# Twelve matmuls whose sums nobody reads, at two waits of TensorE in a gated delta layer

## The chip, the cores and the metric

The program runs on one core of a Trainium2 chip. The metric is the device time of one execution in microseconds (us), here 1743.68 us, the median of three runs. TensorE's clock has two levels, 1.2 and 2.4 GHz; the profile prints the granted clock as a share of the full one, so that 0.50 is the lower level and 1.00 the upper one.

## The reference

Eight layers stand one behind the other, each added to the tokens x (1024 tokens of 256 features): attention, a ternary feed-forward net, gated delta, the ternary net again, attention, routed experts, latent attention, routed experts. The change is in gated delta alone (6 heads, keys of 32 and values of 64 numbers, tokens in chunks):

```
q = short_conv(hidden_states @ Wq, conv_wq)      # k and v alike
beta = sigmoid(hidden_states @ Wb)
g = -exp(A_log) * softplus(hidden_states @ Wa + dt_bias)
def _step(S, xs):                                # one token; q and k normed
    S = S * exp(gt)
    pred = einsum('bhk,bhkv->bhv', kt, S)
    delta = (vt - pred) * bt
    S = S + einsum('bhk,bhv->bhkv', kt, delta)
    return S, einsum('bhk,bhkv->bhv', qt, S)
o = o * rsqrt(mean(o * o) + EPS) * norm_weight * silu(gate)
return o @ Wo
```

## The kernel before

A layer is a row of blocks (`nc.Block()`). Inside a block each engine runs its own list in the order in which it is written, and waits where the code says `wait_ge` on a semaphore. At the end of a block all engines meet, so the next one begins when the last of them is through. No scheduler moves anything. Float32 matmuls are shown in the trace as two records each.

Gated delta works on chunks of 128 tokens, 8 for each of the 6 heads. Its blocks that matter here:

- The factor block (L999 to L1080). VectorE makes decays and norms in a long chain, and from L1076 on the scaled copies of q and k: QN, QE, KN, KB, KBE, KD, 8 instructions each, then BV (L1079). TensorE has two small matmuls in it (L1004, L1005) and is then idle.
- The block of P and A (L1099 to L1196). TensorE transposes the sums of g (L1134), which go to DRAM and come back spread over the partitions (L1104, L1107). It transposes KN, KB and QN in six turns of four (L1130), each copied out by ScalarE (L1158), then makes P and A for 12 units b of four chunks (L1146, matmuls over 32 rows); after each of the first ten units stands one more turn. VectorE multiplies P and A by the decays (L1180 to L1195). When six units of A are written, SyncE carries their 32x32 blocks through DRAM (L833, L836), and GpSimd begins on them in the same block (L1119): steps 0 to 17 of a forward substitution with 31 steps (`substitute`, L820 and L824).
- The block of the merges (L1220 to L1339). GpSimd ends its half, and VectorE does the other half of the blocks (L1329). Each half of the finished T blocks goes through DRAM (L842, L1228, L1231), and TensorE merges blocks of 32 to 64 and 128 (L1260 to L1285) and multiplies by KBE (L1250). `swept[n]` counts two for each step of the substitution of half n.

TensorE's list in the block of P and A begins when all engines have left the factor block; its list in the merges begins with a wait for the first half of the T blocks (L1255).

Of the kernel before, what the change touches and what calls it, by code (L numbers as in the profile page):

```python
# [10 lines left out]
ALU = mybir.AluOpType  # L11
# [3 lines left out]
P = 128  # L15
# [4 lines left out]
HALF = 512  # L20
NH2 = S // HALF
HEADS = 16
HD = D // HEADS
LN_EPS = 1e-5


class Core:
# [13 lines left out]
    def sb(self, name, shape, dt, ctx=None):  # L41
        self.n += 1
        return (ctx or self.ctx).enter_context(self.nc.sbuf_tensor(f"{name}_{self.n}", shape, dt))
# [4 lines left out]
    def sem(self, name):  # L48
        self.n += 1
        self.sems.append(self.nc.alloc_semaphore(f"{name}_{self.n}"))  # L50
        return self.sems[-1]
# [39 lines left out]
def norm_stage(nc, core, tag, loads=None, room=None):  # L91
# [8 lines left out]
    with ExitStack() as tmp:  # L100
# [6 lines left out]
        with nc.Block() as block:  # L107
# [6 lines left out]
            def _(dve):  # L114
                for t in range(NT):
                    dve.bn_aggr(mv[:, t, :], core.stats[:, t, :]).then_inc(mv_done, 1)
                dve.wait_ge(mv_done, NT)
                dve.tensor_scalar(ve[:], mv[:, :, 1], LN_EPS, None, ALU.add).then_inc(var_done, 1)
                dve.wait_ge(std_done, 1)
# [636 lines left out]
GH, GK, GV = 6, 32, 64  # L756
# [4 lines left out]
T32 = 32  # L761
# [7 lines left out]
def gated_delta(nc, core, tag, d):  # L769
# [4 lines left out]
    sem = lambda n: core.sem(f"{tag}_{n}")  # L774
    with ExitStack() as tmp:
        sb = lambda n, shape, dt=F32: core.sb(n, shape, dt, tmp)
        SG = sb("silu_gate", [P, NT, VWD])
        KBE = sb("k_beta_eg", [P, NT, GH, GK])
# [10 lines left out]
        with ExitStack() as mid_scope:  # L789
# [15 lines left out]
            t_eye, swept = sem("t_set_to_identity"), [sem(f"swept_{n}") for n in range(NG)]  # L805
# [43 lines left out]
            with ExitStack() as tmp2:  # L849
# [5 lines left out]
                with ExitStack() as tmp3:  # L855
# [27 lines left out]
                    with nc.Block() as block:  # L883
                        @block.sync
                        def _(sp):
                            sp.wait_ge(wload, 32)
                            sp.wait_ge(head_loads, 32)
# [99 lines left out]
                with ExitStack() as tmp3:  # L987
# [7 lines left out]
                    ss, r = sb3("square_sums", [P, NT, 2 * GH]), sb3("inverse_norms", [P, NT, 2 * GH])  # L995
                    fk = EA[:].rearrange("p c n -> p (c n)")[:, 0:5 * NT * GH].rearrange("p (a t h) -> p a t h", a=5, t=NT)
                    ch, aux, from_act, from_pe = sem("chain"), sem("to_act"), sem("from_act"), sem("from_pe")
                    to_pe, sq_done = sem("to_pe"), sem("sq_done")
                    with nc.Block() as block:  # L999
                        @block.tensor  # L1000
                        def _(pe):
                            pe.wait_ge(to_pe, 1)
                            gf = g[:].rearrange("p t h -> p (t h)")
                            pe.matmul(psum[:, 0, 0:NT * GH], tri[:], gf, start=True, stop=True).then_inc(from_pe, 1)  # L1004
                            pe.matmul(psum[:, 1, 0:NT * GH], core.ones_sq[:], gf, start=True, stop=True).then_inc(from_pe, 1)  # L1005

                        @block.scalar
                        def _(act):
# [15 lines left out]
                        def _(dve):  # L1024
                            n = [0]
# [47 lines left out]
                            for out, src, f in ((QN, q, fk[:, 0]), (QE, q, fk[:, 1]), (KN, k, rk), (KB, k, fk[:, 2]),  # L1073
                                                (KBE, k, fk[:, 3]), (KD, k, fk[:, 4])):
                                for t in range(NT):
                                    dve.tensor_tensor(out[:, t], src[:, t, :].rearrange("p (h c) -> p h c", c=GK),  # L1076
                                                      f[:, t, :].unsqueeze(2).broadcast_to([P, GH, GK]), ALU.mult)
                            for t in range(NT):
                                last = dve.tensor_tensor(BV[:, t], YT[:, t, 2 * QKW:].rearrange("p (h c) -> p h c", c=GV),  # L1079
                                                         beta[:, t, :].unsqueeze(2).broadcast_to([P, GH, GV]), ALU.mult)  # L1080
# [122 lines left out]
            with ExitStack() as tmp2:  # L1203
# [11 lines left out]
                bank = lambda b, i: psum[:, 2 * (b % BANKS) + i, 0:CB * T32].rearrange("p (c n) -> p c n", n=T32)  # L1215
# [4 lines left out]
                with nc.Block() as block:  # L1220
# [18 lines left out]
                    def _(pe):  # L1239
# [14 lines left out]
                        def x32(b):  # L1254
                            pe.wait_ge(placed[((b + 1) * CB - 1) // GCH], 16 * 7)  # L1255
                            if b >= BANKS:
                                pe.wait_ge(y64_kept, b - BANKS + 1)
                            for i, c in enumerate(chunks(b)):
                                for q in (0, 2):
                                    last = pe.matmul(bank(b, 0)[group(q + 1), i], EA[group(q), c, group(q + 1)],  # L1260
                                                     T64[group(q), c, 0:T32], start=True, stop=True)
                            last.then_inc(x_in, 1)
# [19 lines left out]
                        def y64(b):  # L1282
                            pe.wait_ge(x64_kept, b + 1)
                            for i, c in enumerate(chunks(b)):
                                last = pe.matmul(half_bank(b)[lo, i], T64[hi, c], TT[hi, c, hi], start=True, stop=True)  # L1285
                            last.then_inc(y64_in, 1)

                        for b in range(NBT + 2):
                            if b < NBT:
                                x32(b)  # L1290
                            if 1 <= b <= NBT:
                                x64(b - 1)
                            if b < NBT:
                                y32(b)
                            if 1 <= b <= NBT:
                                y64(b - 1)
                            if b >= 2:
                                w_features(b - 2)
# [828 lines left out]
```

## Time and profile before

| what | us |
|---|---|
| median of three runs | 1743.68 (1742.83 to 1750.16) |
| the profiled execution | 1737.53 |
| its span | 1735.7 |
| TensorE busy, of the span | 1464.5 |
| VectorE busy | 979.6 |
| ScalarE busy | 662.2 |
| GpSimd busy | 137.3 |

The busy times are shares of one span and overlap. Times in rows are counted from the start of the span. The page's strip of granted clocks has a digit for each 1/40 of the span (43.4 us); gated delta lies in its slices 9 to 15.

### The profile page before, as it was taken

To read this page: it belongs to the slowest core of one execution; us is meant where nothing else is said; L and a number is where in the kernel's file an instruction comes from. 1 tells how busy PE (TensorE), PEld (TensorE's weight loads), DVE (VectorE), ACT (ScalarE), POOL (GpSimd) and SP (SyncE) were. 2 spreads that over 40 slices of the span, in tenths; PEclk is the share of its full clock that TensorE was granted. 3 is DMA by queue.
4 is the path that set the end of the run, shared out by engine and by line. 5 is a ranking of instruction groups with operands and counts; after the bars stand their busy time and mean duration, and the time that the engine had idled before them with its cause. 6 is when DMAs were issued, how large, how long until landed. Compare 5 with 4: busy or idle time off the path is not lost. (4 is left out here: it accounts for less than half of the span.)

```text
span 1735.7 us, 32934 instructions
## 1 busy us (share of the span) xinstructions
PE 1464.5 (84%) x14035; PEld 838.2 (48%) x14035; DVE 979.6 (56%) x2007; ACT 662.2 (38%) x889; POOL 137.3 (8%) x125
## 2 busy tenths in 40 slices
PE   5799994887192895884799997999888999988998
PEld 3255543363182774362255545435334666655435
DVE  4499966744666425652799944432565555534332
ACT  4077781634222211632377752110362333332110
POOL 4000000000016003003000000110130000000110
PEclk9599997898655697897699998999657999997999
DMA  4900002010042200008500002000320000002000
GB/s 115 152 3 3 3 3 73 0 39 0 1 109 50 38 4 0 1 25 151 69 3 3 3 1 86 0 1 1 58 37 10 9 10 10 9 13 76 0 1 25
DMA packets 54952, 51.78 MB, mean 30 GB/s; under 512 B 23843, under 2 KB 41110, under 8 KB 54806
## 3 DMA queue, kind: packets, MB, share of 16 engines
q1 hardware_dynamic: 54806, 49.68, 13.9%
q8 instruction: 111, 1.82, 0.4%
q14 instruction: 35, 0.29, 0.1%
HBM read 36.66 MB, written 9.72 MB: 27 GB/s over the span
## 5 line engine op out<-in xcount | busy, mean ns | idle before, releaser
L453 DVE TENSOR_REDUCE row_max_pieces<-psum 128x1 f32<-128x512 f32 x704 | 425.3, 648 | 145.2 <-PE psum L368 143.5
L519 ACT ACTIVATE probs<-psum 128x1024 f32<-128x1024 f32 (+7 forms) x384 | 343.7, 900 | 297.8 <-PE psum L368 297.7
L425 PE MATMUL psum<-probs,v_ones 128*32 128x256 f32 (+1 forms) x2688 | 238.2, 375 | 2.3 <-ACT out_features L510 1.7
L368 PE MATMUL psum<-q_all,k_head 97*32 97x512 f32 (+3 forms) x1536 | 207.3, 494 | 0.0
L368 PE MATMUL psum<-k_stack,q_stack 96*32 96x512 bf16 x2048 | 174.6, 409 | 27.2 <-PEq L583 26.4
L368 PE MATMUL psum<-q_stack,k_stack 97*32 97x512 bf16 x2048 | 160.0, 384 | 6.6 <-DMA q_stack<-minus_max_rows 6.6
L425 PEld LDWEIGHTS psum<-probs,v_ones 128*32 128x32 f32 x2688 | 85.9, 109 | 59.6 <-issue 14.2
L368 PEld LDWEIGHTS psum<-k_stack,q_stack 96*32 96x32 bf16 x2048 | 59.3, 97 | 101.2 <-issue 29.9
L368 PE MATMUL psum<-k_head_bf,q_all_bf 80*32 80x512 bf16 (+3 forms) x768 | 101.7, 347 | 7.3 <-DMA k_head_bf<-k_features_bf 6.9
L368 PEld LDWEIGHTS psum<-q_stack,k_stack 97*32 97x32 bf16 x2048 | 58.3, 97 | 58.4 <-DMA q_stack<-minus_max_rows 7.6
L1716 DVE TENSOR_TENSOR gate_weighted<-psum,weight_rows 128x512 f32<-128x512 f32 (+1 forms) x48 | 33.1, 690 | 89.4 <-PE psum L1624 89.4
L368 PEld LDWEIGHTS psum<-q_all,k_head 97*32 97x32 f32 x1536 | 71.1, 111 | 15.9 <-issue 1.4
L1657 ACT ACTIVATE silu<-psum 128x512 f32<-128x512 f32 (+1 forms) x48 | 28.6, 596 | 131.3 <-PE psum L1624 131.3
L248 PE MATMUL psum<-xn_parts,w_up_signs 128*128 128x512 bf16 x192 | 49.2, 395 | 20.0 <-DVE xn_parts L295 20.0
L368 PE MATMUL psum<-mask_by_key,identity_bf 128*32 128x128 bf16 x512 | 63.6, 221 | 0.0
L134 ACT ACT_TABLE_LOAD x7 | 9.0, 1283 | 141.2 <-PEq L62 132.1
L368 PE MATMUL psum<-mask_by_query,identity_bf 128*32 128x128 bf16 x512 | 59.2, 231 | 0.0
L368 PEld LDWEIGHTS psum<-k_head_bf,q_all_bf 80*32 80x32 bf16 x768 | 39.4, 99 | 37.9 <-issue 10.4
L1735 PE MATMUL psum<-slot_hidden,down_a 128*128 128x512 f32 (+1 forms) x96 | 47.5, 644 | 6.3 <-PEq L1556 6.3
L1624 PE MATMUL psum<-lora_in,up_b 128*128 128x512 f32 (+1 forms) x96 | 49.9, 601 | 3.4 <-DVE lora_in L1703 3.4
L1848 PE MATMUL psum<-latents,w_q_rotary 64*128 64x512 f32 x64 | 51.0, 977 | 1.2 <-DVE by_cos_over_by_sin L1931 1.2
L151 PE MATMUL psum<-identity,xn 128*128 128x128 f32 x96 | 23.0, 428 | 32.2 <-DVE xn L124 32.2
(334 smaller groups left out, 2286.6 us busy)
## 6 DMA issues: line engine op xcount, KB each, us to landing
aa_parts<-qk_parts SPq DMA_DIRECT2D x12, 256.0 KB, 12.5
q_stack<-aa_parts SPq DMA_DIRECT2D x12, 256.0 KB, 8.5
k_stack<-aa_parts SPq DMA_DIRECT2D x12, 256.0 KB, 17.7
e_then_minus_a<-gd_g_sums SPq DMA_DIRECT2D x6, 512.0 KB, 7.3
ac_parts<-qk_parts SPq DMA_DIRECT2D x12, 256.0 KB, 11.9
q_stack<-ac_parts SPq DMA_DIRECT2D x12, 256.0 KB, 8.7
k_stack<-ac_parts SPq DMA_DIRECT2D x12, 256.0 KB, 18.6
w_up<-in_r_up SPq DMA_DIRECT2D x2, 704.0 KB, 4.7
```

The lines of the kernel that those rows point to most:

```text
L134: act.activation(std[:], ve[:], ACT.Sqrt).then_inc(std_done, 1)
L151: last = pe.transpose(psum[:, 2 * half + f, i * P:(i + 1) * P], xn[:, t, f * P:(f + 1) * P], ident[:])
L248: last = pe.matmul(psum[:, 2 * b + j, :], w[:, k, e * P:(e + 1) * P], XP[:, part, k, cols(half)], start=(part == 0 and k == 0), stop=(part ...
L368: last = pe.matmul(o[j:j + 32], by[:, j:j + 32], rows, **flags)
L425: last = pe.matmul(psum[32 * g:32 * g + VW, PVB, a - g * D:D], V[:, c, h, :], pr[:, n % PB, a:(g + 1) * D], start=(c == 0), stop=(c == (2 ...
L453: dve.reduce_max(mx[:, h % 2, qt, i:i + 1], psum[:, RB + n % RING, 0:b - a], AX.X).then_inc(ring_out, 1)
L519: act.activation(pr[:, n % PB, q_from(c):], psum[:, 2 * (n % 2):2 * (n % 2) + 2, :].rearrange("p a n -> p (a n)")[:, q_from(c):], ACT.Exp, ...
L1624: pe.matmul(psum[0:n, 2 * (p % BUF) + j, :], w[wl][:, a:a + n], Z[:, j, k, cols], start=False, stop=True, skip_group_check=True).then_inc( ...
L1657: act.activation(sil[0:n, i % 2, :], psum[0:n, 2 * (p % BUF), :], ACT.Silu).then_inc(silu, 1)
L1716: dve.tensor_tensor(gc[0:n, i % 2, :], psum[0:n, 2 * (p % BUF) + 1, :], CB[0:n, k, cols], ALU.mult).then_inc(gated, 1)
L1735: last = pe.matmul(psum[:, 2 * half + k, :], w["dnA"][0:n, f, :], H[0:n, k, f, half * HALF:(half + 1) * HALF], start=(f == 0), stop=(f == ...
L1848: last = pe.matmul(o, wq[:, n - 1, :], L[0:LAT, cols(half)], start=True, stop=True)
```

## The change

A helper issues n matmuls of 128x512 from the identity and the normed tokens, both long in place, into a PSUM bank that nobody reads before it is written anew. Six of them stand at the end of TensorE's list in the factor block, behind a wait for the last instruction that writes KBE. Six more stand at the head of its list in the merges, behind a wait for step 29 of the first half's substitution (`swept[0]` at 60 of 63).

```
+def keep_busy(pe, core, bank, n):
+    for _ in range(n):
+        pe.matmul(core.psum[:, bank, :], core.ident[:], core.XNT[:, 0, 0:HALF], start=True, stop=True)
...
-                    to_pe, sq_done = sem("to_pe"), sem("sq_done")
+                    to_pe, sq_done, scaled = sem("to_pe"), sem("sq_done"), sem("k_decayed_made")
...
                             pe.matmul(psum[:, 1, 0:NT * GH], core.ones_sq[:], gf, start=True, stop=True).then_inc(from_pe, 1)
+                            pe.wait_ge(scaled, 1)
+                            keep_busy(pe, core, 2, 6)
...
                                 for t in range(NT):
-                                    dve.tensor_tensor(out[:, t], ...
+                                    last = dve.tensor_tensor(out[:, t], ...
+                                if out is KBE:
+                                    last.then_inc(scaled, 1)
...
+                        pe.wait_ge(swept[0], 2 * (T32 - 2))
+                        keep_busy(pe, core, 7, 6)
                         for b in range(NBT + 2):
```

TensorE's list from the two matmuls of the factor block to the transposes of the block of P and A, before (P is made from qn_features, A from kb_features):

```order
L1004 MATMUL psum<-g,upper_ones 128x48
L1005 MATMUL psum<-g,ones_square 128x48
L999 UNCONDITIONAL_BRANCH
L1121 UNCONDITIONAL_BRANCH
L1134 MATMUL psum<-identity,g_sums 48x128
L1130 MATMUL psum<-identity,k_normed 128x128 x8
```

The same place now, where every line number has grown by 6 to 10:

```order
L1010 MATMUL psum<-g,upper_ones 128x48
L1011 MATMUL psum<-g,ones_square 128x48
L30 MATMUL psum<-xn_features,identity 128x512 x6
L1005 UNCONDITIONAL_BRANCH
L1131 UNCONDITIONAL_BRANCH
L1144 MATMUL psum<-identity,g_sums 48x128
L1140 MATMUL psum<-identity,k_normed 128x128 x8
```

Six matmuls (L30) now stand ahead of the branch that ends the block, and so ahead of the transpose of the sums of g. TensorE's list from the last unit of P and A to the first merges, before:

```order
L1146 MATMUL psum<-kb_features,kn_features 128x128 x4
L1099 UNCONDITIONAL_BRANCH
L1238 UNCONDITIONAL_BRANCH
L1260 MATMUL psum<-t_first_half,e_then_minus_a 32x32 x24
L1267 MATMUL psum<-a_times_t,t_inverse_transposed 32x32 x12
```

The same place now:

```order
L1156 MATMUL psum<-kb_features,kn_features 128x128 x4
L1109 UNCONDITIONAL_BRANCH
L1248 UNCONDITIONAL_BRANCH
L30 MATMUL psum<-xn_features,identity 128x512 x6
L1270 MATMUL psum<-t_first_half,e_then_minus_a 32x32 x24
L1277 MATMUL psum<-a_times_t,t_inverse_transposed 32x32 x12
```

The six stand inside the new block, ahead of the first merges. VectorE's list is the same but for one signal.

## Rows read from the trace of the kernel before

**Rows 1.** The page's strip of granted clocks, 40 slices of the span.

```profile
PEclk9599997898655697897699998999657999997999
```

**Rows 2.** Stretches: length, busy us of each engine (instructions), granted clock, DMA.

```profile
473.90:477.70 3.80, 3.79 (x18) 3.19 (x19) 0.00 (x0) 2.06 (x4) 0.00 (x0) 0.50 0.08 22
477.80:481.10 3.30, 2.46 (x19) 1.99 (x20) 0.63 (x4) 3.01 (x4) 0.00 (x0) 1.00 1.00 290
481.20:533.00 51.80, 51.71 (x222) 44.85 (x221) 34.36 (x80) 12.26 (x22) 16.44 (x30) 0.50 0.30 71
533.00:565.70 32.70, 0.00 (x0) 0.00 (x0) 19.00 (x42) 7.20 (x4) 19.03 (x34) 0.50 0.35 69
584.60:597.20 12.60, 12.57 (x186) 11.76 (x188) 2.88 (x5) 2.35 (x4) 0.00 (x0) 0.50 0.01 3
597.30:616.00 18.70, 17.23 (x296) 15.50 (x292) 3.55 (x5) 8.77 (x15) 0.00 (x0) 1.00 0.01 2
```

**Rows 3.** Timeline of the handover: start, us, engine, line, [idle before <-releaser].

```profile
465.48 2.23 DVE L1076 TENSOR_TENSOR k_beta_eg<-conv_tokens,e_then_minus_a 128x192 f32<-128x192 f32 x8
...
469.77 3.83 DVE L1079 TENSOR_TENSOR beta_v<-conv_tokens,beta 128x384 f32<-128x384 f32 x8
...
473.91 0.38 PE L1134 MATMUL psum<-identity,g_sums 128*48 128x128 f32 x1 [22.88 <-PEq L999]
...
474.08 1.92 PE L1130 MATMUL psum<-identity,k_normed 128*128 128x128 f32 x8
...
478.48 0.66 PE L1130 MATMUL psum<-identity,q_normed 128*128 128x128 f32 x4 [0.15 <-ACT kb_features L1158]
479.17 0.60 ACT L1158 ACTIVATE qn_features<-psum 128x512 f32<-128x512 f32 x1 [0.21 <-PE psum L1130]
...
479.82 1.15 PE L1146 MATMUL psum<-qn_features,kn_features 32*128 32x128 f32 x8 [0.69 <-ACT qn_features L1158]
480.47 1.66 DVE L1180 TENSOR_SCALAR e_then_minus_a<-e_then_minus_a,g_sums 128x128 f32<-128x128 f32 x8 [6.87 <-DMA e_then_minus_a<-gd_g_sums]
```

**Rows 4.** Timeline of units of P and A, and what follows the sixth.

```profile
502.11 2.07 PE L1146 MATMUL psum<-qn_features,kn_features 32*128 32x128 f32 x8
...
506.00 0.69 DVE L1195 SCALAR_TENSOR_TENSOR e_then_minus_a<-psum,e_then_minus_a 128x512 f32<-128x512 f32 x1 [1.02 <-PE psum L1146]
...
506.72 2.10 SPq L833 DMA_DIRECT2D gd_a_blocks<-e_then_minus_a  x4
506.81 1.78 PEld L1146 LDWEIGHTS psum<-qn_features,kn_features 32*128 32x128 f32 x8 [0.38 <-issue]
...
514.29 0.23 POOL L820 TENSOR_TENSOR outer_products<-minus_a_blocks,t_blocks 96x31 f32<-96x31 f32 x1 [130.50 <-DMA minus_a_blocks<-gd_a_blocks]
```

**Rows 5.** Timeline from GpSimd's early half to the merges.

```profile
537.35 0.67 POOL L824 TENSOR_TENSOR t_blocks<-t_blocks,outer_products 96x252 f32<-96x252 f32 x1
538.34 2.08 SPq L833 DMA_DIRECT2D gd_a_blocks<-e_then_minus_a  x4
...
546.01 0.46 DVE L820 TENSOR_TENSOR outer_products<-minus_a_blocks,t_blocks 96x31 f32<-96x31 f32 x1 [12.30 <-DMA minus_a_blocks<-gd_a_blocks]
...
551.94 0.30 POOL L824 TENSOR_TENSOR t_blocks<-t_blocks,outer_products 96x60 f32<-96x60 f32 x1
...
565.74 1.49 PE L1260 MATMUL psum<-t_first_half,e_then_minus_a 32*32 32x32 f32 x48 [32.83 <-DMA t_first_half<-gd_t_blocks]
...
584.63 1.49 PE L1260 MATMUL psum<-t_first_half,e_then_minus_a 32*32 32x32 f32 x48 [0.74 <-DMA t_first_half<-gd_t_blocks]
```

**Rows 6.** Timeline: four 128x512 matmuls (8 records) at the upper clock.

```profile
396.38 3.60 PE L903 MATMUL psum<-xn_features,e_then_minus_a 128*128 128x512 f32 x8
```

**Rows 7.** Stretches elsewhere, ahead of and behind a change of clock (columns as rows 2).

```profile
1161.00:1163.80 2.80, 2.77 (x4) 1.25 (x5) 0.00 (x0) 0.00 (x0) 0.00 (x0) 0.50 0.00 0
1163.90:1165.00 1.10, 1.10 (x4) 0.45 (x3) 0.00 (x0) 0.00 (x0) 0.00 (x0) 1.00 0.00 0
...
1222.70:1228.60 5.90, 5.90 (x7) 2.38 (x8) 4.76 (x3) 0.00 (x0) 0.13 (x1) 0.50 1.03 109
1228.70:1229.40 0.70, 0.59 (x2) 0.00 (x0) 0.70 (x1) 0.08 (x1) 0.00 (x0) 1.00 0.68 70
```

**Rows 8.** Stretches behind TensorE's last work of an earlier block (columns as rows 2).

```profile
438.90:443.60 4.70, 0.03 (x1) 0.00 (x0) 3.69 (x4) 3.53 (x6) 0.00 (x0) 1.00 0.00 0
443.70:447.00 3.30, 0.00 (x0) 0.00 (x0) 3.27 (x2) 0.00 (x0) 0.00 (x0) 0.50 0.00 0
```

More of the change, by code:

```diff
@@ L1075, in _ @@
                                 for t in range(NT):
-                                    dve.tensor_tensor(out[:, t], src[:, t, :].rearrange("p (h c) -> p h c", c=GK),
-                                                      f[:, t, :].unsqueeze(2).broadcast_to([P, GH, GK]), ALU.mult)
+                                    last = dve.tensor_tensor(out[:, t], src[:, t, :].rearrange("p (h c) -> p h c", c=GK),
+                                                             f[:, t, :].unsqueeze(2).broadcast_to([P, GH, GK]), ALU.mult)
+                                if out is KBE:
+                                    last.then_inc(scaled, 1)
                             for t in range(NT):
```

## The prediction

> **What bounds the kernel now.** I read the strip of granted clocks first [rows 1]: TensorE is the busiest engine, and its clock is at the upper level in most slices, but slices 11 to 14, in the gated delta layer, show 0.5 and 0.6. I then cut that layer into stretches [rows 2]. The reader is to see there a stretch of 51.8 us, the units of P and A, in which TensorE is busy for 51.7 us at 0.50, then 32.7 us in which it has nothing to do, and a stretch of 12.6 us in the merges, busy all the time, at 0.50 again; from 597.3 on it is at 1.00. So two stretches are bound by a slow TensorE, and a higher clock there would shorten them. The timeline gives the pace: a unit of P and A takes 4.70 us (502.11 to 506.81 [rows 4]), while VectorE works 34.36 us on the 12 units, 2.9 us each [rows 2].
>
> Which wait ends last tells how far a saving goes. SyncE carries the A blocks off as soon as the sixth unit is written (506.00 + 0.69, then 506.72 [rows 4]); GpSimd starts at 514.29 on them [rows 4], its 18th step ends at 538.02, the block ends with it, and SyncE's next transfer starts at 538.34 [rows 5]. TensorE has been through since 533.0. From there the chain is the transfer, VectorE's substitution from 546.01, another transfer, and the merges of the second half at 584.63 [rows 5]. So what TensorE gains or loses up to the sixth unit moves everything behind it, one for one; what it gains in units 7 to 12 is lost in the wait for GpSimd.
>
> **The six ahead of P and A: the delay.** They start when KBE is written: 465.48 + 2.23 = 467.7 [rows 3]. Four such matmuls are eight records in 3.60 us at the upper clock, the last alone 0.6 by its own length (its loading included), so 0.43 for each further record [rows 6]; at the lower clock seven records fill 5.90 us, 0.84 each, which I round to 0.86 as twice 0.43 [rows 7]. Six matmuls are 12 records: 5.1 us at the upper clock, 10.3 at the lower. They start at 0.50, since TensorE has been idle. How long they stay there I bound by three places where it began after a pause: 2.8 us of work before the clock rose [rows 7], 3.8 here [rows 2] and 6.0 in the stretch from 1222.7 [rows 7]. A stretch of c us at half clock costs c/2, so the six take 5.1 + c/2, 6.5 to 8.1 us, and end at 474.3 to 475.9; with c in the middle, 4.4, at 475.1. VectorE ends the block before at 473.6 (469.77 + 3.83), and TensorE goes on 0.3 us later, at 473.9 [rows 3]. So the six are hidden for their first 5.8 us by VectorE's KD and BV, and the rest delays the transpose of the sums of g and all behind it, its trip through DRAM included: 0.7 to 2.3 us, I take 1.5.
>
> **What the six give.** First, the six turns of transposes run wholly at the upper clock. In the trace the first eight records take 1.92 us at 0.50, where four take 0.66 at 1.00 [rows 3]. But behind each turn stands ScalarE's copy of 0.60 us [rows 3], and with two banks the turns go no faster than the copies let them, some 0.85 us a turn; worked through turn by turn this brings the first unit of P 0.4 us nearer to the block's start (bounds 0 and 0.8). Second, the clock falls later. In the trace it falls at 481.2 [rows 2], 2.0 us behind the last transpose (478.48 + 0.66 [rows 3]) and 1.35 us into the first unit, in spite of TensorE being busy with units from 479.8 on; and all 51.8 us of units behind it stay at 0.50. Elsewhere it fell 4.7 us behind the last work [rows 8]. So it will fall 2.0 to 4.7 us behind the last transpose, 0 to 2.7 us later than it does now, and each us of upper clock in a stretch that TensorE bounds does the work of two and saves one: 0 to 2.7, I take 1.5, a little over the middle, since TensorE is then at the upper clock from the start of the transposes. VectorE, with 2.9 us of work in each 4.7, is able to follow from the second unit on.
>
> Sum of the first edit: +1.5 - 0.4 - 1.5 = -0.4 us. At the ends: 0.7 - 0.8 - 2.7 = -2.8, and +2.3 - 0 - 0 = +2.3.
>
> **The six ahead of the merges.** Their wait is satisfied at 551.94 + 0.30 = 552.2 [rows 5]. By the same reckoning they end at 558.8 to 560.4, and the first merges start at 565.74, released by a transfer [rows 5]: at least 5.3 us later. So they delay nobody, in a stretch in which TensorE had nothing to do [rows 2]. But the pause behind them is longer than the 4.7 us after which the clock had fallen in rows 8, so the merges start at 0.50 as before. And the merges that decide, the busy 12.6 us from 584.63, lie 19 us further on. I take 0. Below nothing: 0 to -0.2 if the first merges still catch the upper clock, since their second half waits for a transfer that starts from VectorE anyway. Above nothing: no bank, semaphore or engine is shared, 0. The extra signal on VectorE's last KBE instruction costs nothing that a row shows.
>
> At one place the Trainium skill speaks against me. Rows 2 and 3 show that from 473.9 to 477.7 TensorE did nothing but transposes, and the clock then rose. "TensorE: Matmul & The Clock Gate", Part 4 on the transpose, says that transposes do not count as busy in the same way and do not raise the clock. By that rule the clock of the changed kernel would fall during the transposes; the trace before disagrees, and the measurement decides. It is a rival below all the same.
>
> **The number.** Against the profiled execution, 1737.53 us with a span of 1735.7, the sum is -0.4: 1737.1. The runs shown lie higher, 1742.83 to 1750.16, by scatter that this change doesn't touch, so from their median: 1743.68 - 0.4 = 1743.3. A measurement of this kernel can tell about 0.5% from no change, 8.7 us; all my terms together are a third of that.
>
> **Rivals.**
>
> A, the clock holds. If a TensorE that enters the units at the upper clock kept it there, units 1 to 6 would go at VectorE's pace with its waits, about 3.2 us instead of 4.7: 5 x 1.5 = 7.5 us less up to the sixth. If also the merges from 584.63 were at 1.00, their 12.6 us would be 6.3. Less the 1.5 of delay and 0.4 gained in transposes: -12.7, a time of 1731. For it: the merges from 597.3 do keep the upper clock, with gaps [rows 2]. Against it: at 481.2 the clock was at 1.00 when the units came, and it fell with TensorE busy; and 19 us at low load lie between the second six and the merges that count. Units alone, without the merges, give -6.4, 1737.
>
> B, the clock doesn't rise in time, the rival on the slower side. If the six ran at 0.50 throughout, 12 x 0.86 = 10.3 us, they would end at 478.1, 4.5 us behind VectorE; from c = 1.4 us on any us of lower clock is already half a us of delay. If the rise then came as late in the transposes as to be lost on the first unit, 1.35 more: +5.9, a time of 1749.6. Against it: 128x512 matmuls raised the clock in 2.8 and 6.0 us [rows 7], and the six last longer than that.
>
> C, transposes don't hold the clock (the mechanism of the rule above). It would fall 2.0 to 4.7 us behind the six, at 477.1 to 479.8, before the first unit: 1.5 of delay, 0.2 gained in the first transposes, and 1.35 lost where the first unit now has the upper clock: +2.6, 1746.3.
>
> D, the change is neutral because the delay is hidden: the next block's first transpose waits on VectorE's end anyway. It would ask for six matmuls in under 5.8 us, and 5.1 us need the upper clock from the first record on. Then -1.9, 1741.8. TensorE had been idle for 16 us, so this has next to no chance.
>
> **How the numbers follow.** My forecast has 0.80, A 0.07 (half of it reaching beyond 0.5%), B 0.05, C 0.06, D 0.02. The likeliest case has its own range of -2.8 to +2.3, 1740.9 to 1746.0; A and B widen it, and the median of the next runs carries the scatter of the ones shown (1742.83 to 1750.16, and the profiled one at 1737.53), so 1737 to 1749. Faster by over 0.5%: 0.08, from A and from scatter. Slower: 0.04, from B with scatter. Within: 0.88.
>
> **What would show it.** In the profile of the changed kernel: 12 records at L30 from 467.8 on, the first of them 0.86 apart and the later ones 0.43; the transpose of the sums of g at 474.5 to 476.2 in place of 473.9; all transposes at 1.00; units of P and A again 4.7 us apart at 0.50 from the second on; a second group from 552, over before 561, a clock of 0.50 when the first merges start, and again from 584 on until KBE is multiplied. It is wrong if the clock is at 1.00 for more than one or two units, if the first unit starts more than 2.3 us late, or if the merges begin at 1.00.

## The result, and the profile after

The changed kernel took 1750.09 us (median of 20 runs, 1741.91 to 1783.1), the kernel before, in 20 runs, 1742.3 us. The ratio is 1.0054, with a 95% interval of 1.0034 to 1.0074: slower by 0.54%, about 9 us. I had forecast 1743.3 us and no change. (Some executions of most kernels are disturbed and take some 20 to 40 us longer; the ratios leave them out, and the profiles of two experiments, three matmuls and the first run of six small ones, are of that kind.)

The profiled execution of the changed kernel took 1749.24 us with a span of 1747.3, 11.6 us more than the span before. First the page: busy times, strip of clocks, DMA queues.

```profile
PE 1483.0 (85%) x14051; PEld 848.9 (49%) x14059; DVE 980.4 (56%) x2007; ACT 662.8 (38%) x889; POOL 137.2 (8%) x125
...
PEclk9599997998655597897699998999757999998999
...
q1 hardware_dynamic: 54806, 49.68, 13.9%
q8 instruction: 111, 1.82, 0.4%
```

Against [rows 1] slices 12 to 16 read 5, 5, 5, 9, 7 in place of 5, 5, 6, 9, 7, and there are small differences further on. The strip is too coarse to say more. The line that I did not read before is the one of queue q8: the program itself comes over the DMA engines.

The timeline of the first group and what follows it (start, us, engine, line; the line numbers are 10 higher than before):

```profile
467.88 6.96 PE L30 MATMUL psum<-xn_features,identity 128*128 128x512 f32 x12 [16.74 <-DVE k_beta_eg L1084]
...
475.14 0.27 PE L1144 MATMUL psum<-identity,g_sums 128*48 128x128 f32 x1 [0.30 <-PEq L1005]
475.25 1.03 PE L1140 MATMUL psum<-identity,k_normed 128*128 128x128 f32 x8
...
477.88 1.14 PE L1140 MATMUL psum<-identity,q_normed 128*128 128x128 f32 x8 [0.20 <-ACT kb_features L1168]
...
479.71 1.15 PE L1156 MATMUL psum<-qn_features,kn_features 32*128 32x128 f32 x8 [0.69 <-ACT qn_features L1168]
```

The six take 6.96 us where I had 6.5 to 8.1, and the transpose of the sums of g comes at 475.14 instead of 473.91 [rows 3], 1.2 us late. But the first unit starts at 479.71, 0.11 us earlier than before: the transposes at the upper clock gave all of it back. The stretches of the clock (length, busy us of each engine, granted clock, DMA share, GB/s) and the units:

```profile
471.30:481.20 9.90, 8.46 (x47) 5.38 (x46) 2.56 (x7) 4.81 (x8) 0.00 (x0) 1.00 0.29 86
...
481.30:533.00 51.70, 51.31 (x221) 44.45 (x219) 35.36 (x84) 12.38 (x22) 15.59 (x29) 0.50 0.32 76
...
563.20:566.50 3.30, 0.00 (x0) 0.00 (x0) 3.06 (x8) 0.00 (x0) 0.00 (x0) 0.50 0.87 109
```

```profile
501.81 2.07 PE L1156 MATMUL psum<-qn_features,kn_features 32*128 32x128 f32 x8
...
506.42 2.12 SPq L839 DMA_DIRECT2D gd_a_blocks<-e_then_minus_a  x4
506.51 1.86 PE L1156 MATMUL psum<-qn_features,kn_features 32*128 32x128 f32 x7
```

The clock falls at 481.3 (481.2 before), the units stand 4.70 us apart at 0.50 (501.81 to 506.51), and all of them are 0.3 us earlier than before. So TensorE's part of the P and A block has cost nothing, and TensorE is through with it at 533 as before. The second group and the merges:

```profile
553.03 7.06 PE L30 MATMUL psum<-xn_features,identity 128*128 128x512 f32 x12 [20.42 <-POOL t_blocks L830]
...
566.50 1.49 PE L1270 MATMUL psum<-t_first_half,e_then_minus_a 32*32 32x32 f32 x48 [6.42 <-DMA t_first_half<-gd_t_blocks]
...
581.21 1.66 SPq L1241 DMA_DIRECT2D t_first_half<-gd_t_blocks  x3
...
585.96 1.49 PE L1270 MATMUL psum<-t_first_half,e_then_minus_a 32*32 32x32 f32 x48 [1.29 <-DMA t_first_half<-gd_t_blocks]
...
595.39 4.50 PE L1260 MATMUL psum<-t_inverse_transposed,k_beta_eg 128*32 128x128 f32 x24
...
623.20 1.52 PE L1384 MATMUL psum<-beta_v,t_inverse_transposed 128*128 128x64 f32 x12 [0.93 <-PEq L1230]
```

The six of the second group are over at 560.09, 6.4 us before the first merges, and the clock is at 0.50 again from 563.2, as foreseen. Yet the second half's merges start at 585.96 instead of 584.63 [rows 5], and the sweep over the state, the next block, at 623.20, where the kernel before has it at 616.57:

```profile
616.57 1.52 PE L1372 MATMUL psum<-beta_v,t_inverse_transposed 128*128 128x64 f32 x12 [0.93 <-PEq L1220]
```

So 6.6 of the 11.6 us are gone by 623: 1.3 us before the second half's merges start, and 5.3 us in them, where no instruction was changed (37.24 us from their start to the sweep, 31.94 before). Two readings say how.

**The 5.3 us are the clock.** Stretches of the changed kernel from the start of the second half's merges:

```profile
585.90:600.50 14.60, 14.54 (x218) 13.21 (x220) 2.60 (x4) 3.52 (x6) 0.00 (x0) 0.50 0.00 1
600.70:603.90 3.20, 3.20 (x112) 3.09 (x108) 0.00 (x0) 1.77 (x3) 0.00 (x0) 0.99 0.03 5
604.10:610.70 6.60, 6.60 (x53) 5.65 (x47) 2.60 (x4) 1.18 (x2) 0.00 (x0) 0.50 0.01 2
610.90:614.20 3.30, 2.40 (x36) 2.02 (x34) 0.00 (x0) 1.40 (x2) 0.00 (x0) 0.99 0.00 0
614.40:617.50 3.10, 3.10 (x24) 2.73 (x22) 0.95 (x1) 0.00 (x0) 0.00 (x0) 0.50 0.00 0
```

Before, the clock rose 12.6 us into the merges and stayed up [rows 2]. Here it rises only 14.8 us into them, falls again twice (at 604.1 and 614.4), and is up for good from 617.8. The work between is the same.

**The 1.3 us begin in two transfers.** The first is the store of the A blocks behind the sixth unit, which GpSimd's chain starts from. SyncE begins to issue it at 506.42 (0.30 us earlier than before), and its next issue, the load of the same blocks, which waits for the store, stands at 511.71, where it was at 511.01. So the store takes 5.29 us instead of 4.29. The traffic from 506.7 to 511 before (the GB/s line has 40 slices of the stretch), and from 506.4 to 511.7 in the changed kernel:

```profile
GB/s 0 0 0 0 0 0 0 0 95 202 211 186 156 88 110 110 110 104 111 86 57 52 50 68 144 200 219 211 213 192 174 156 133 108 105 9 0 0 0 0
...
q1 hardware_dynamic: 3136, 0.39, 62.3%
```

```profile
GB/s 0 0 0 0 0 0 38 185 213 177 120 103 110 105 227 98 57 49 60 116 180 201 204 200 167 147 128 106 42 14 12 12 11 12 1 0 0 0 0 0
...
q1 hardware_dynamic: 3136, 0.39, 50.8%
q8 instruction: 1, 0.02, 1.4%
```

In the changed kernel one packet of q8, a 16 KB piece of TensorE's program, travels among the A blocks. Behind the main traffic comes a tail of 0.7 us at 11 to 14 GB/s. That is about a sixteenth of the 200 to 220 GB/s at the peaks, so I read it as one of the 16 DMA engines, which still carries the packets that stood behind the piece of program; the trace does not name the engine. The packet in the store goes with the 1.0 us, which is still there at 566.50, 0.76 behind [rows 5] after a start 0.3 ahead.

The second transfer is the load of the second half's T blocks. From the end of its last issue to the merges go 2.54 us before (580.43 + 1.66 to 584.63) and 3.09 us after (581.21 + 1.66 to 585.96). Its issue in the trace before, and the traffic from 580.4 to 584.6:

```profile
580.43 1.66 SPq L1231 DMA_DIRECT2D t_first_half<-gd_t_blocks  x3
```

```profile
GB/s 198 198 184 169 154 159 159 146 184 187 188 155 138 123 160 160 173 177 172 165 162 172 166 205 165 146 143 151 126 89 71 44 6 0 0 0 0 0 0 0
...
q1 hardware_dynamic: 4187, 0.52, 93.0%
```

and the same of the changed kernel, 581.2 to 585.9:

```profile
GB/s 134 140 186 184 191 115 130 162 192 172 112 129 247 134 161 147 167 167 185 191 165 177 151 184 153 117 88 30 17 11 13 14 13 13 14 13 14 5 0 0
...
q1 hardware_dynamic: 4032, 0.51, 74.0%
q8 instruction: 1, 0.02, 1.8%
```

The same again: one packet of q8, and a tail of 1 us at 11 to 14 GB/s. The kernel before has that piece just behind its load, at 585.7, when the merges have begun: from 584.7 to 590 its trace has that one packet and nothing else.

```profile
DMA packets 1, 0.02 MB, mean 3 GB/s; under 512 B 0, under 2 KB 0, under 8 KB 0
...
q8 instruction: 1, 0.02, 1.1%
```

There are 111 such pieces for 14051 matmul records and as many loads, so one for about 256 instructions of TensorE. Six float32 matmuls are 12 records and 12 loads, 24 instructions; the pieces do not change in number, but each now ends 24 instructions earlier in the work, and behind the second group 48. "Runtime: NRT & Kernel Launch", Terms, in the Trainium skill, says of an engine's instruction memory that it is refilled in blocks of 16 KiB; the packets in the trace agree (1.82 MB in 111). The kernels below with 64 more matmuls, 256 instructions, have 112 packets of q8 in place of 111.

The rest of the 11.6 us, about 5, comes later. By the starts of the same matmuls in both traces the lag grows in four pieces of 1.2 to 2 us, in the first three of which the clock is low for longer in the changed kernel than in the one before; 1.6 us come back near 1580, where it is the other way round. One piece, in the changed kernel and then at the same work in the one before:

```profile
1034.30:1037.50 3.20, 3.15 (x15) 3.19 (x16) 0.00 (x0) 1.52 (x3) 0.00 (x0) 0.50 0.00 0
```

```profile
1025.00:1028.10 3.10, 2.59 (x20) 2.41 (x20) 0.19 (x2) 1.93 (x4) 0.00 (x0) 1.00 0.00 0
```

### The profile page after: what moved, and what is told of

Read it like the earlier page. It is cut to its first block and busy times, and to the rows that moved or that the text cites. A ratio compares the mean times of both kernels' runs of the same rounds, so it can differ in the third digit from the quotient of the medians.

```text
span 1747.3 us, 32974 instructions
## 1 busy us (share of the span) xinstructions
PE 1483.0 (85%) x14051; PEld 848.9 (49%) x14059; DVE 980.4 (56%) x2007; ACT 662.8 (38%) x889; POOL 137.2 (8%) x125
## 3 DMA queue, kind: packets, MB, share of 16 engines
q1 hardware_dynamic: 54806, 49.68, 13.9%
q8 instruction: 111, 1.82, 0.4%
## 5 line engine op out<-in xcount | busy, mean ns | idle before, releaser
L157 PE MATMUL psum<-identity,xn 128*128 128x128 f32 x96 | 22.6, 424 | 32.2 <-DVE xn L130 32.2
## 6 DMA issues: line engine op xcount, KB each, us to landing
aa_parts<-qk_parts SPq DMA_DIRECT2D x12, 256.0 KB, 12.2
```

What stands on the lines that cost most here:

```text
L157: last = pe.transpose(psum[:, 2 * half + f, i * P:(i + 1) * P], xn[:, t, f * P:(f + 1) * P], ident[:])
```

## The experiments

My theory was formed in two steps, and the first four runs came before the second. It is that the loss is no work at all: the added instructions move the pieces of program, one of which then delays the T blocks, and the merges, started about 1 us later, meet the moments at which the clock can change in another place. The rivals: the first group's delay of 1.2 us, the second group, or the matmuls' own work. Each ratio is against the kernel before on the same chip, but three chips were used: one for the first four experiments (each group alone, three matmuls, before again), a second for the first run of six small ones, the changed kernel with 52, the second group with 58 and one sum, a third for the other four.

**Each group alone.** The change with the second group left out:

```diff
-                        pe.wait_ge(swept[0], 2 * (T32 - 2))
-                        keep_busy(pe, core, 7, 6)
```

> Only the six matmuls ahead of P and A; the six ahead of the merges are left out. The changed kernel measured 0.54% slower than before (1750.1 against 1742.3 us). Theory 1 (edges of the clock): the grid on which the clock can change stands nearly still against the program's start, and a shift of the merges by 1 to 2 us moves their strong matmuls across an edge; the shift comes from the first group, so this kernel keeps most of the loss, +5 to +9 us. Theory 2 (the second group costs): TensorE's work in the wait ahead of the merges disturbs them or what follows; then this kernel is within 2 us of before. Theory 3 (delay alone): it costs what its delay of TensorE costs, 0 to 2.3 us.

Measured: 1749.71 us, ratio 1.0051 (1.0034 to 1.0069). And with the first left out:

```diff
-                            pe.wait_ge(scaled, 1)
-                            keep_busy(pe, core, 2, 6)
...
-                                if out is KBE:
-                                    last.then_inc(scaled, 1)
```

> Only the six matmuls ahead of the merges. Theory 1: they delay nobody and the clock falls before the merges start, so the edges stand as before: within 2 us of before. Theory 2: +5 to +9 us. Theory 3: 0.

Measured: 1751.6 us, ratio 1.0062 (1.0039 to 1.0085). Each alone costs as much as both. No sum of two costs does that, and the second group is over 6 us before anything needs TensorE. None of the three theories had both results: the first expected nothing of the second group, the second nothing of the first, the third at most 2.3 us of either. Both profiles have the piece of program in the T load. From the first group alone, 582 to 587.4:

```profile
GB/s 155 134 180 174 213 155 137 156 188 165 121 88 115 134 159 162 210 207 172 178 176 184 282 97 47 11 7 1 0 0 0 7 8 9 9 9 3 0 0 0
...
q1 hardware_dynamic: 4237, 0.53, 69.9%
q8 instruction: 1, 0.02, 1.3%
```

Its merges start 3.71 us behind the last issue's end, and the clock in them does what it does in the changed kernel:

```profile
587.50:601.50 14.00, 14.00 (x200) 12.63 (x202) 2.60 (x4) 3.04 (x6) 0.00 (x0) 0.50 0.00 1
602.10:605.00 2.90, 2.90 (x98) 2.79 (x92) 0.00 (x0) 1.77 (x3) 0.00 (x0) 1.00 0.03 6
605.50:611.40 5.90, 5.90 (x49) 5.04 (x44) 2.60 (x4) 0.88 (x2) 0.00 (x0) 0.50 0.00 0
```

**Three in the first group**, and no second:

```diff
-                            keep_busy(pe, core, 2, 6)
+                            keep_busy(pe, core, 2, 3)
```

> Only the first group, with three matmuls in place of six, which end before VectorE's 473.6 and so delay nobody, but still raise the clock early: the first unit of P starts up to 0.5 us sooner. Theory 1: the merges shift by less than 1 us to the early side; within 3 us of before, of either sign, as their edges decide. Theory 3: -0.5 to -2 us, a small gain, since the delay is gone and the higher clock is left. Theory 2: -0.5 to -2 us as well.

Measured: 1744.47 us, ratio 1.0016 (0.9994 to 1.0039). With 12 added instructions the piece comes at 585.2, behind the start of the merges at 584.31. But another piece lies in the store of the A blocks, which takes 5.78 us here, the longest of all:

```profile
504.94 2.11 SPq L839 DMA_DIRECT2D gd_a_blocks<-e_then_minus_a  x4
...
510.72 0.32 SPq L842 DMA_DIRECT2D minus_a_blocks<-gd_a_blocks  x1
```

So a piece in that store alone does not seem to bring the whole loss. Only places and lengths of this kind are taken from its profile.

**The kernel before once more**, unchanged, for the scatter:

> The kernel before, unchanged, for the scatter and for the place of the clock's edges in another execution. Theory 1 in its strict form: the edges lie within 0.5 us of where they lie in the two profiles that exist (0.76 and 0.98 us in the trace's own count, which agree to 0.2 us). If they lie anywhere, the grid does not stand still, and a steady loss of 7.8 us cannot come from one unlucky edge. Time within 2 us of before in either case.

Measured: 1740.78 us, ratio 1.0007 (0.9986 to 1.0028). Its profile, though, taught most: with a span of 1745.3 us it shows the same loss in the merges, 38.4 us to the sweep, with the clock rising 14.6 us into them, though its piece of program is behind the T load (at 589.7, the merges from 588.70). So the loss in the merges and the piece of program are two things; the second is one way into the first.

**Only the instructions.** Six matmuls of 32x32, no work worth naming, where TensorE waits at the head of the factor block:

```diff
+def fill_code(pe, core, n):
+    for _ in range(n):
+        pe.matmul(core.psum[0:32, 2, 0:32], core.ident[:, 0:32], core.XNT[:, 0, 0:32], start=True, stop=True)
...
+                            fill_code(pe, core, 6)
                             pe.wait_ge(to_pe, 1)
```

> No matmul that keeps TensorE busy at either wait: six matmuls of 32x32, as many instructions as one group of the change, stand at the head of TensorE's list in the factor block, where it waits 10 us. They take under 2 us there and delay nobody; all that changes is where the later instructions of TensorE lie in its code, which is fetched in pieces of 16 KB over the queue q8. Theory 4 (code): in the three slow kernels so far (both groups, first alone, second alone) a piece was fetched just ahead of the merges of the second half, while the T blocks were on their way, and those ended 0.6 to 1.4 us later; a shift of six matmuls alone does it too, and the late start costs more in the merges, as the clock then rises one edge later: +5 to +9 us, the whole loss. Theory 1 with a delay from TensorE's work, and theory 2 (the second group's own work): 0, within 2 us of before.

Measured: 1779.93 us in 6 runs, with one of 1745.19; too few count for a ratio. The profile shows the piece at 588.3 among the T blocks, and 3.75 us from the last issue's end to the merges (585.63 + 1.66 to 591.04). Run again:

> The kernel before with six 32x32 matmuls at the head of the factor block, in a wait of TensorE: no work worth naming, only 24 more instructions in TensorE's code. Theory (code and clock edges): a piece of TensorE's code is fetched while T blocks travel to the second half's merges, these begin about 1 us later and meet the fall and rise of the clock badly: 1747 to 1753 us beside 1742 of before, ratio 1.003 to 1.007; last T-load issue's end to first merge 3.1 to 3.8 us instead of 2.5. Rival (the loss is the work of 128x512 matmuls, their heat or their port): no difference, ratio 0.999 to 1.001.

Measured: 1743.46 us, ratio 1.0007 (0.9981 to 1.0034). I had expected 1.003 to 1.007, so this is a miss, and the profile says where:

```profile
580.22 1.67 SPq L1238 DMA_DIRECT2D t_first_half<-gd_t_blocks  x3
...
585.92 1.49 PE L1267 MATMUL psum<-t_first_half,e_then_minus_a 32*32 32x32 f32 x48 [2.24 <-DMA t_first_half<-gd_t_blocks]
```

```profile
585.90:599.00 13.10, 13.08 (x189) 12.18 (x190) 2.60 (x4) 2.36 (x4) 0.00 (x0) 0.50 0.00 1
599.60:630.00 30.40, 28.36 (x389) 24.84 (x388) 7.91 (x17) 8.95 (x15) 0.00 (x0) 1.00 0.02 6
```

The T load is the latest of all, its merges 4.03 us behind the last issue's end. But the clock rises 13.5 us into the merges and stays: they take 32.4 us. The piece of program in the T load is there in all five profiles with 24 or 48 instructions added ahead of it and in no other; what it costs seems to depend on where the clock's change then falls.

**The program filled up to a whole piece.** 58 small matmuls with either group, 52 with both, make 64 added matmuls ahead of the merges, 256 instructions, and put every piece behind them back to its place in the work. With both groups:

```diff
+                            fill_code(pe, core, 52)
                             pe.wait_ge(to_pe, 1)
```

> The changed kernel with 52 small matmuls of 32x32 at the head of the factor block, so that 64 are added in all ahead of the merges: 64 float32 matmuls are 256 instructions, one whole piece of 16 KB, and the merges lie in their pieces as before. The small ones take 5 to 8 us of a wait of 10 us. Theory 4: the fetch is again behind the start of the second half's merges, and the loss goes: within 2 us of before (-1 to +2, the delay of the first group stays). Theory 2: the loss stays, +6 to +9.

Measured: 1740.89 us, ratio 1.0002 (0.9984 to 1.0019). The traffic from 583.4 to 587.7 has no packet of q8, and the clock rises once:

```profile
GB/s 161 166 188 197 196 181 98 122 155 149 188 157 167 114 129 158 191 184 193 182 187 191 204 167 154 154 164 137 95 66 41 10 6 0 0 0 0 0 0 0
...
q1 hardware_dynamic: 4164, 0.52, 88.1%
```

```profile
587.70:600.40 12.70, 12.69 (x188) 11.85 (x189) 2.79 (x5) 2.35 (x4) 0.00 (x0) 0.50 0.01 3
600.90:630.00 29.10, 27.06 (x382) 23.69 (x380) 7.33 (x16) 9.40 (x16) 0.00 (x0) 1.00 0.02 6
```

The second group with 58:

> Only the second group of the change, and 58 small matmuls at the head of the factor block, 64 in all ahead of the merges. Theory 4: within 1.5 us of before, where the second group alone cost 0.62%. Theory 2: +6 to +10 us as before.

Measured: 1740.76 us, ratio 0.9997 (0.9979 to 1.0016). The first group with 58:

> The first six 128x512 matmuls of the change, with 58 small ones at the head of the factor block, so that 64 are added in all, a whole piece of code; the second six left out. Theory: all fetches stand at the same places of the work as in the kernel before; what is left is the first group's own effect on time, near 0: ratio 0.999 to 1.001, 1740 to 1744 us. Rival (the first group's delay of 1.2 us is what costs): ratio as with the first group alone, 1.003 to 1.007.

Measured: 1736.56 us, ratio 0.9992 (0.9967 to 1.0016). That makes three pairs whose kernels differ by nothing but small matmuls in a wait: 1.0054 and 1.0002, 1.0062 and 0.9997, 1.0051 and 0.9992. In each the kernel with more instructions has the lower ratio, and in each the intervals are apart. The work of the groups and their delay are kept (with 58 the first group takes 8.40 us, from 471.07, and the transpose of the sums of g starts at 479.77), the small matmuls take under 4 us at the head of a wait, and the loss is gone. In the three profiles no piece lies in either transfer: the store takes 4.28 to 4.29 us, and the merges start 2.51 to 2.60 us behind the last issue's end. This speaks for the place of the program's pieces and against the groups' own work. It is no proof, for no pair was measured on one chip: each group alone ran on the first of the three chips, the filled kernels on the other two, and the chip of the changed kernel's own runs is not on record. That the other two would not have shown the loss without filling was not tested with a group, and on the third the six small matmuls cost nothing that could be measured. On the second the next run shows that the merges can lose time.

**A later start without any change in TensorE's program.** VectorE sums rows of the T blocks once, behind its substitution of the second half, 1.2 us:

```diff
+                    if n == 1:
+                        eng.reduce_sum(outer[:, n, 0:T32], TB[:, n], AX.X)
                     eng.tensor_copy(MA[:, n], TB[:, n].rearrange("p t j -> p j t")).then_inc(step, 1)
```

> The kernel before with one extra VectorE instruction of 1.1 us at the end of its substitution, ahead of the store of the second half's T blocks; TensorE's list is the same. It puts the merges of the second half 1.1 us later and nothing else. Edges theory: the first multiplication by KBE then begins too late to raise the clock at the edge at which it now does, the clock rises one edge later and falls once more in the merges: +5 to +7 us for a delay of 1.1. Plain delay: +1.1 us.

Measured: 1754.76 us in 9 runs, ratio 1.0087 (1.0056 to 1.0118): 15 us by the ratio, 12 by the medians, where the sum's own length is 1.2 and I had expected 5 to 7. That is also more than the 6.5 us that the merges lost in any profile. The profiled execution, at 1745.65 the quickest of the nine, met the clock well (13.2 us into the merges) and so doesn't show the loss; the times do, and where it lies stays open. Three sums in place of one:

```diff
+                        for r in range(3):
+                            eng.reduce_sum(outer[:, n, T32 * r:T32 * (r + 1)], TB[:, n], AX.X)
```

> The kernel before with three sums of rows behind VectorE's substitution of the second half (1.1 to 1.2 us each): the merges of the second half are 3.4 to 3.6 us later, code of TensorE unchanged. Theory (clock edges, which come at equal distances): one such sum cost 15 us, since it moved the merges across an edge; three move them by nearly the whole distance of two edges, so the clock rises at the same place of the work again, and the cost is the delay itself: +2 to +5 us, ratio 1.001 to 1.003, less than one sum alone. Rival (a later start is simply paid for, with some factor): three cost more than one, ratio over 1.0087.

Measured: 1744.23 us, ratio 1.0034 (1.0009 to 1.0059). The sums took 3.47 us:

```profile
575.21 3.47 DVE L830 TENSOR_REDUCE outer_products<-t_blocks 96x32 f32<-96x1024 f32 x3
```

Three times the delay costs less than half as much. The intervals overlap a little, at 1.0056 and 1.0059, and the two were measured on different chips, so it is likely and not certain that more delay cost less. A delay that is simply paid for wouldn't do that; moments of change that come round again would. 5.9 us (0.34%) is above what I expected, 2 to 5: in its profile the clock rises a little too early, 11.8 us into the merges, and falls once.

**Six small matmuls behind the merges**, at the start of the state's sweep:

```diff
                         u_from_v(0)
+                        fill_code(pe, core, 6)
```

> The kernel before with the six 32x32 matmuls behind the merges, at the start of the state's sweep, where TensorE waits for VectorE to set the state to zero. Theory with the fetch beside the T load as the only cause: the fetches up to the merges stay where they were, ratio 0.999 to 1.001. Theory with later fetches taking part as well (all behind the merges shift by 24 instructions): up to half of the loss, ratio 1.001 to 1.003. Rival (any six more matmuls cost this): 1.003 to 1.007.

Measured: 1744.49 us, ratio 1.0014 (0.9989 to 1.0039). Up to the merges its pieces are where they were (90.1% of the T load's stretch is q1's, no q8), and the ratio is below those of the groups but does not exclude a part of the loss further on. Its profiled execution met the merges badly, at 38.4 us, as the second one of the kernel before did.

**The store of the A blocks in all 14 profiles.** From its first issue to the load's: 4.28 to 4.30 us in the nine where no packet of q8 lies between (before, before again, second alone, second + 58, first + 58, changed + 52, one sum, three sums, six small behind), and 5.09 to 5.78 in the five where one does (changed 5.29, first alone 5.39, six small 5.09 and 5.48, three of the first 5.78). The second group stands behind this store in the program and cannot move the piece in it, and with the second group alone the store takes 4.30. The wait from the last issue of the T load to the merges goes the same way: 2.4 to 2.7 us in the nine profiles without a packet of q8 in it, 3.1 to 4.0 in the five with one (changed, first alone, second alone, six small twice). Of all readings here these are the sharpest: one piece of program, 0.5 to 1.5 us.

**The merges in all 14 profiles.** Us from the start of the second half's merges to the rise of the clock, and to the start of the sweep; read from stretches and timelines as above:

| kernel | to the rise | to the sweep |
|---|---|---|
| three sums | 11.8 | 35.7 |
| first + 58 | 12.2 | 33.0 |
| second + 58 | 12.3 | 33.0 |
| before | 12.6 | 31.9 |
| changed + 52 | 12.9 | 32.1 |
| one sum | 13.2 | 32.2 |
| six small, again | 13.5 | 32.4 |
| three of the first | 13.5 | 35.1 |
| six small, first run | 13.9 | 35.2 |
| first alone | 14.3 | 38.2 |
| before again | 14.6 | 38.4 |
| second alone | 14.7 | 38.4 |
| six small behind | 14.75 | 38.4 |
| changed | 14.8 | 37.2 |

The merges take 32 to 33 us when the clock rises 12.2 to 13.5 us into them (three of the first apart), 35 to 36 at 11.8 and 13.9, and 37 to 38 when it comes after 14.3 us or more: the multiplication with KBE, which starts 9.4 us in and is 3.7 to 4.5 us long, is then over. It alone uses all 128 rows; what follows is 32x32 and 64x64 work again, in which the clock fell in each of the profiles from 14.3 us on. So I read it as a matter of where a moment of change falls against one long multiplication.

The direction is worth a line. A start of the merges that is later by 1.3 us brings a fixed moment of change nearer to it, from 12.6 to 11.3 us. But in no profile did the clock rise before 11.8 us, 2.4 us into that multiplication. The changed kernel missed that moment and rose at a later one, 14.8 us in.

## Why the prediction was wrong

**The first group's delay.** Right in size (1.5 us, measured 1.2). The transposes gave back more than the 0.4 I took, and more than my bound of 0.8: 1.3 us, all of the delay and 0.1 on top, since a turn took 0.66 us (four turns from 475.25 to 477.88) where I had taken 0.85. The clock's fall did not move, and gave 0.2 us in place of the 1.5 that I had taken. Measured up to the sixth unit: 1.2 - 1.3 - 0.2 = -0.3 us. My sum was -0.4, and it came near by luck: two of its three terms were wrong by about 1 us each, in opposite directions. The units stayed 4.7 us apart, as predicted; rival A did not come.

**Transposes and the clock (rival C).** The clock held at 1.00 from 471.3 to 481.2, through all the transposes. The Trainium skill, "TensorE: Matmul & The Clock Gate", Part 4, says that TensorE's transpose mode does not count as busy in the same way. The transposes of this kernel held the clock here, and raised it before (477.8, behind 3.8 us of them [rows 2]); weighing the trace above the page was right. Whether they use that mode the trace does not say.

**The second group.** Its times were right: over at 560.1, the clock down at 563.2, the merges begun at 0.50. The step that failed is the sentence "Above nothing: no bank, semaphore or engine is shared, 0". Two things are shared that are no bank, semaphore or engine of computation: the DMA engines, which also carry the pieces of the program, each of them moved by added instructions, and the chip's moments of clock change. The first put 16 KB into the transfer that ends last before the merges (2.5 us from the last issue became 3.1 to 4.0). The second made of about 1 us a loss of 5.3 in the merges of the changed kernel's profile, and 6.2 and 6.5 in those of the groups alone. The first group's instructions do the same, and put another piece into the store of the A blocks, 1.0 us: so its account, right as far as the sixth unit, was not complete either.

**The merges.** "The merges that decide lie 19 us further on. I take 0" treated the rise of the clock at 597.2 as a property of the merges. It depends on where the merges start: 12.2 to 13.5 us are good, 14.3 and more are bad, and the profile of the kernel before stands at 12.6, only 0.8 us above the earliest rise of all 14 profiles, 11.8. A later start takes just that away, and the clock then rises at a later moment. A row that shows the clock rising once shows one draw, and I should have asked what a start 1 us later would do to it. A part of the price could then have been estimated from the kernel's own rows: a clock that rises only behind the KBE multiplication leaves it at half speed.

**The range.** 1737 to 1749 was made from known terms and scatter; the term that came out had no place in it. My chance of 0.04 for slower was far too low for a change that puts 48 instructions into a program whose stages wait for transfers.

**Why a scattered clock gives a steady loss.** If the moments of change were met by chance, the loss would be noise. They are not: early in the span the profiles have the first fall of the clock anywhere from 34.9 to 38.1 us, but at 440 us, counted from one and the same instruction to the moment of change behind it, 10 of the 14 lie within 0.2 us of one another and the other four 0.5 us off, within 0.02 of one another. The Trainium skill, "TensorE: Matmul & The Clock Gate", Part 1, says that the window in which the chip looks at activity is free-running and does not start with the kernel; the scatter at the start agrees. That the kernel's long stages, whose pace depends on the clock, bring it into step, and that this makes most executions alike, is my reading of 14 profiles; no run forced it.

**What stays open.** Why six small matmuls alone have a ratio of 1.0007 while either group has 1.005 to 1.006, with the same packet in the T load. The profiles point at the clock (13.5 us against 14.3 to 14.8 into the merges), but each is one execution, and the interval of the one, up to 1.0034, touches those of the others. As no kernel with a group was measured with and without filling on one chip, a difference between chips is the rival that is left. It is not known where the 12 to 15 us of one sum lie. Nor was it tried which of the later places (near 829, 1034 and 1230 us) are moved by pieces of program and which by the 6.6 us of shift alone.

## What to carry to other kernels

Instructions that do nothing may not be free, even in a wait: they move every later piece of the program, and a piece may land in the transfer that something waits for. So look at the instruction queue's packets beside the last transfer before a stage, and when an edit costs what its work can't explain, fill the program up to a whole piece and measure again, both kernels on one chip. Where a stage depends on a clock that rises in it, ask what a start one us later would do, before calling a small delay small.

## What the runs showed of the hardware

- A 16 KB packet of TensorE's program takes 0.9 to 2.1 us (14 profiles); among small packets (4032 of them carry 0.51 MB) it goes with a tail at 11 to 14 GB/s. The store of the A blocks went from 4.3 us to 5.1 to 5.8, the wait for the T blocks from 2.4 to 2.7 us to 3.1 to 4.0.
- The loss did not grow with the program's length: with 24 or 48 instructions added by the groups it was 0.5 to 0.6%, with 256 there was none that could be measured (0.9992 to 1.0002 in three kernels, on other chips).
- Nor, it seems, with the delay: 1.2 us ahead of the merges cost 0.87% on one chip, 3.5 us cost 0.34% on another.
- Executions of one and the same kernel can differ by 6 us in one stage with nothing changed (31.9 and 38.4 us in two profiles of the kernel before).
- No version beat the kernel before by more than can be measured; the best median, 1736.56 us, has a ratio of 0.9992 (0.9967 to 1.0016).
